# Attention products of a 3x3 convolution over 128 partitions, 5 for 6, with one read of x

## The reference

```python
x = x + L0(gn(x)); x = x + L1(gn(x)); x = x + L2(gn(x)); x = x + L3(gn(x))

def L0(x):                       # attention over channels, one head
    qkv = conv1x1(x, qkv_w)      # 48 -> 144 channels
    qkv = depthwise3x3(qkv, dw_w)
    q, k, v = split(qkv, 3)      # each (b, 48, h*w)
    q, k = l2_normalize(q), l2_normalize(k)
    attn = softmax(q @ k.T * temperature)      # 48 x 48
    return conv1x1(attn @ v, proj_w)
```

## Time and profile before

| | |
|---|---|
| median of 3 runs | 2777.19 us (2773.39 to 2782.19) |
| profiled execution | 2774.55 us |
| its span | 2772.4 us |
| TensorE busy | 2579.3 us (93%) |
| VectorE / ScalarE / GpSimd busy | 1492.3 / 1005.3 / 423.7 us |
| mean granted clock | 0.979 |

### The profile page before, as it was taken

How to read it: one execution, slowest core, us unless ns; L and a number is a source line. 1 busy time by engine, 2 the same in 40 slices (tenths; PEclk the granted TensorE clock), 3 DMA queues, 4 the chain that set the end, 5 groups by cost and what they waited for, 6 DMA issues and landing times.

```text
span 2772.4 us, 48058 instructions
## 1 busy us (share of the span) xinstructions
PE 2579.3 (93%) x18728; PEld 2244.8 (81%) x18728; DVE 1492.3 (54%) x3683; ACT 1005.3 (36%) x2608; POOL 423.7 (15%) x492
## 2 busy tenths in 40 slices
PE   1999999999999989999999998999999999877896
PEld 1999948954599559999999998999999999763443
DVE  3323323322333235677656787656776557876765
ACT  3524344354433334443344333344433443212221
POOL 1000000000300009400000235500000003563230
PEclk9999999999999999999999999999999999988998
DMA  8850000003000134000000436600000003657233
GB/s 150 146 87 4 1 0 1 1 1 87 4 1 1 23 68 48 2 2 1 2 1 2 92 64 121 92 1 1 2 2 1 2 2 70 169 136 219 79 103 91
DMA packets 245089, 130.32 MB, mean 47 GB/s; under 512 B 209152, under 2 KB 234080, under 8 KB 241856
## 3 DMA queue, kind: packets, MB, share of 16 engines
q1 hardware_dynamic: 243808, 126.52, 22.1%
q10 hardware_dynamic: 928, 0.76, 0.1%
q0 software_dynamic: 128, 0.01, 0.0%
HBM read 76.91 MB, written 50.33 MB: 46 GB/s over the span
## 4 chain that ended last, share of the span: by engine, by line
PE 84%; DVE 8%; SPq 2%; issue 2%; ACT 2%; DMA 1%; POOL 0%; ACTq 0%; DVEq 0%; POOLq 0%
PE bank L1057 16%; PE bank L1060 15%; PE bank L1058 15%; PE bank L950 14%; PE bank L1009 12%; PE bank L968 3%; PE bank L955 3%; PE bank L1199 2%; SPq L493 2%; PE bank L1141 1%; PE bank L1079 1%; DVE work L389 1%; DMA work<-in_x 1%; DVE stats L1222 1%; DVE bank L1416 1%
## 5 line engine op out<-in xcount | busy, mean ns | idle before, releaser
L1416 DVE TENSOR_SCALAR bank<-image,scan_bias 112x128 f32<-112x128 f32 x2032 | 706.9, 353 | 428.6 <-ACT image L809 400.6
L809 ACT COPY image<-bank 112x128 f32<-112x128 f32 x2032 | 546.1, 269 | 1031.8 <-PE bank L1060 920.2
L1057 PE MATMUL bank<-image,scan_wt 112*112 112x128 f32 x4064 | 810.5, 280 | 41.8 <-ACT image L809 39.6
L1058 PE MATMUL bank<-image,scan_wt 112*112 112x126 f32 x4064 | 770.7, 271 | 0.0
L1060 PE MATMUL bank<-image,scan_wt 112*112 112x126 f32 x4064 | 770.3, 270 | 0.0
L1057 PEld LDWEIGHTS bank<-image,scan_wt 112*112 112x112 f32 x4064 | 560.1, 175 | 98.9 <-ACT image L809 73.1
L1058 PEld LDWEIGHTS bank<-image,scan_wt 112*112 112x112 f32 x4064 | 581.2, 176 | 0.0
L1060 PEld LDWEIGHTS bank<-image,scan_wt 112*112 112x112 f32 x4064 | 578.6, 176 | 0.0
L755 ACT ACTIVATE work<-image,gn_shift,gn_scale 48x567 f32<-48x567 f32 (+3 forms) x384 | 335.1, 902 | 324.9 <-PE bank L955 202.2
L950 PE MATMUL bank<-work 112*128 112x192 f32 x2304 | 421.6, 331 | 10.1 <-issue 10.1
L950 PEld LDWEIGHTS bank<-work 112*128 112x128 f32 x2304 | 373.4, 192 | 11.6 <-issue 11.3
(11 more groups left out here) (140 smaller groups left out, 1516.9 us busy)
## 6 DMA issues: line engine op xcount, KB each, us to landing
work<-saved SPq DMA_DIRECT2D x64, 192.0 KB, 5.1
saved<-image SPq DMA_DIRECT2D x64, 192.0 KB, 4.0
work<-saved SPq DMA_DIRECT2D x128, 96.0 KB, 3.5
flat_rows<-work SPq DMA_DIRECT2D x64, 192.0 KB, 3.7
image<-flat_rows SPq DMA_DIRECT2D x4, 3072.0 KB, 14.5
out<-image SPq DMA_DIRECT2D x8, 1536.0 KB, 9.3
band<-in_x SPq DMA_DIRECT2D x16, 384.0 KB, 5.5
work<-in_x SPq DMA_DIRECT2D x16, 384.0 KB, 5.5
```

The source lines that it names most:

```text
L809: nc.scalar.copy(line(g, along_w, at), state_bank(g, done)).then_inc(s_state[g], 1)
L1057: mm(dst, wt[:, 1], src, start=False, stop=False, skip_group_check=True)
L1058: mm(dst[:, 1:J2, :], wt[:, 0], src[:, 0:J2 - 1, :], start=False, stop=False, skip_group_check=True)
L1416: v.tensor_scalar(state_bank(g, done), line(g, along_w, src), scan_bias[:, 3 * layer + kind:3 * layer + kind + 1], None, ALU.add).then_inc ...
```

## The change

- **128 partitions.** The spare partitions of `blk_z` get the n rows of channels 32 to 47, of both parities, by two DMAs a block on SP's queue (`tail`). They wait for `s_stage`, and their signal is `s_tail`.
- **Packed side columns.** `blk_2` holds the side columns of channels 0 to 31 for three rows on 96 partitions. For every block of every stage VectorE packs them in two turns (`pack(k, turn)`, five copies each), each after the near pieces of ScalarE (`s_near`) and with the signal `s_pack`.
- **Five products for six**: three over `blk_z` and two over `blk_2`. In QK0 that is 3 of 192 columns and 2 of 96 for 6 of 192; in QK1 to QK3 for 4 and 2; in CV 5 of 512 for 6.
- TensorE waits at a block's start for `s_stage`, `s_tail` and `s_pack` (`block_ready`). ScalarE writes the n pieces first, then the z pieces.
- **x is read once.** Six loads are started at once. For image 0 ScalarE copies the even and the odd part, for the others ScalarE the even and GpSimd the odd one. The norm of image 1 moves to the middle of QK0, that of images 2 and 3 into QK1. The small constants are spread behind the tails.

```diff
+        TAPS = [(LO, 0, 1), (slice(0, HALF), 1, 0), (slice(HALF, 128), 0, 2), (HI, 1, 1)]
...
+            def tail(k):
+
+                m = k % 2
+                sp.wait_ge(s_stage, k + 1)
+                sp.dma_start(blk_z[m][C:HALF, :], blk_n[m][SPARE, :]).then_inc(s_tail[m], 16)
+                sp.dma_start(blk_z[m][HALF + C:128, :], blk_n[m][HALF + 32:P, :]).then_inc(s_tail[m], 16)
...
+            for k in range(NBLK, 2 * NB * NBLK):
+                tail(k)
...
+                if k == CV_AT[1] + NBLK + 2:
+                    sp.wait_ge(s_x1, TWO + 2 * 2 * NBLK)
+                    for t in range(2):
+                        for half, rows in enumerate((LO, HI)):
+                            sp.dma_start(saved[0][half, :, t * IMG:(t + 1) * IMG],
+                                         image[rows, t * IMG:(t + 1) * IMG]).then_inc(s_save[t], 16)
...
             def split(c):
-                m, b, k0 = c % 2, c // LOADS, c % LOADS * BLK
-                act.wait_ge(s_load[m], 32 * (c // 2 + 1))
...
+                _, sem_at, n = rows_of(c)
+                act.wait_ge(s_load[sem_at], n)
+                last = nc.scalar.copy(*split_rows(c, False))
+                if c < LOADS:
+                    last = nc.scalar.copy(*split_rows(c, True))
+                last.then_inc(s_split, 1)
...
+                if i == 0 and k >= 2:
+                    act.wait_ge(s_pack, 2 * k - 2)
+                    act.wait_ge(s_tail[m], 32 * (k // 2))
+                elif i == 4:
+                    block_free(act, k)
+                sub, piece = i % 2, (1, 2, 0)[i // 2]
...
+            def block_ready(k):
+                pe.wait_ge(s_stage, k + 1)
+                pe.wait_ge(s_tail[k % 2], 32 * (k // 2 + 1))
+                pe.wait_ge(s_pack, 2 * k + 2)
...
+                    block_ready(first + n)
                     for sub in range(2):
 
                         pe.wait_ge(s_x1, b * 2 * NBLK + TWO + 2 * n + sub + 1 - len(banks))
-                        prods = [(buf, dy, s, dk) for buf in range(2) for dy, s, dk in conv_rows(sub)]
...
+                        for dy, s, dk in conv_rows(sub):
                             o = s * ZSUB + (1 + dk) * J2
...
+                            mm(dst, out_w[:, dy, :], blk_z[n % 2][:, o:o + BLK * J2], start=(dy == 0), stop=False)
+                            if beats is not None and dy != 1:
                                 beats()
+                        for side in range(2):
+                            last = mm(dst, out_w2[:, side, :], blk_2[n % 2][:, side, sub, :], start=False, stop=(side == 1))
+                        last.then_inc(s_conv, 1)
...
+            def pack(k, turn):
+
+                if k >= 2 * NB * NBLK:
+                    return
+                m, side = k % 2, 1 - turn
+                if turn == 0:
+                    block_free(dve, k)
+                dve.wait_ge(s_near, 2 * k + turn + 1)
...
+            def add_blocks(b, then):
                 for n in range(NBLK):
                     end = n == NBLK - 1
...
+                    for sub in range(2):
+                        last = add_part(b, n, sub, None if end else CV_AT[b] + n + 2, bank_out)
+                        if end and sub == 1:
+                            last.then_inc(s_stat, 1)
+                        pack(CV_AT[b] + n + 1, sub)
                     then(n)
```

More of the change, by code:

```diff
@@ L264, in build @@
         s_stage = sem("s_stage")
+        s_near = sem("s_near")
         s_pack = sem("s_pack")
+        s_tail = [sem(f"s_tail{m}") for m in range(2)]
         s_qk = sem("s_qk")
@@ L439, in _, with save_part @@
                         for m in shifts:
[L440 to L450, removed]
+                            small.append((scan_wt[rows, t, m + 1, cols], scan_w[t][:, 2 * m + qi - qo + 2, :], s_scan_c))
+            assert len(small) == N_GATE + N_SCAN_DMA
+            def save_part(i):
                 sp.wait_ge(s_x1, TWO + (NB - 1) * 2 * NBLK + (i + 1) * 2 * NBLK // PARTS)
@@ L729, in stage_piece @@
             def stage_piece(phase, n, i):
[L731 to L739, removed]
-                kk0, rows = 1 - sub, BLK + 1
[L741 to L748, removed]
+                b, m, k = ORDER[phase][1], n % 2, phase * NBLK + n
+                if i == 0 and k >= 2:
[4 more added lines that the diff above has]
+                sub, piece = i % 2, (1, 2, 0)[i // 2]
+                kk0, rows = 1 - sub, BLK + 1
+                outer = {0: 1, NBLK - 1: 0}.get(n)
+                if outer is not None:
+                    if i in (0, 4):
+                        o = outer * ZSUB + (0 if outer else BLK + 1) * J2
+                        nc.scalar.copy((blk_n, blk_z)[i // 4][m][0:P, o:o + J2], zero_row)
+                    if sub == outer:
+                        rows = BLK
+                        kk0 += n == 0
                 buf, part, d, e = ((blk_z, slice(0, P), (0, J2), (0, J2)), (blk_n, LO, (0, J2 - 1), (1, J2)),
@@ L938, in conv_pair @@
                     if i % 4 == 0:
-                        pe.wait_ge(s_stage, stages + (n + 1))
-                        if packed is not None:
-                            pe.wait_ge(s_pack, packed + (2 * n + 2))
+                        block_ready(first + n)
                     pe.wait_ge(s_qk_sb, pairs + (i + 1))
@@ L995, in tap_weights, with output_conv @@
                 for t in range(9):
-                    last = mm(bank_wt[0:P, t * C:(t + 1) * C], v_taps[:, t, :], mix_t, start=True, stop=True)
+                    last = mm(bank_wt[:, t * C:(t + 1) * C], v_taps[:, t, :], mix_t, start=True, stop=True)
                 last.then_inc(s_sm_t, 1)
-            def output_conv(b, stages, behind={}, banks=bank_out, beats=None):
+            def output_conv(b, first, behind={}, banks=bank_out, beats=None):
                 pe.wait_ge(s_outw, b + 1)
@@ L1001, in output_conv @@
                 for n in range(NBLK):
[L1002 removed]
+                    block_ready(first + n)
                     for sub in range(2):
                         pe.wait_ge(s_x1, b * 2 * NBLK + TWO + 2 * n + sub + 1 - len(banks))
[L1006 to L1007 removed]
+                        dst = banks[(2 * n + sub) % len(banks)][0:P, :]
+                        for dy, s, dk in conv_rows(sub):
```

336 lines of the change are left out of this document (203 added, 133 removed).

## The result

| | before | after |
|---|---|---|
| median | 2775.93 us (4 runs, 2773.39 to 2782.19) | 2809.11 us (4 runs, 2805.52 to 2817.29) |
| profiled execution, its span | 2774.55, 2772.4 | 2806.22, 2804.4 |
| TensorE busy | 2579.3 | 2495.5 |
| mean granted clock | 0.979 | 0.951 |

The ratio is 1.0119, 95% interval 1.0103 to 1.0134: the change made the kernel slower by 33 us. The prediction, 2770 with a range to 2806, had the sign wrong (about no change, leaning to faster) and missed the top of its range by 3 us. TensorE has 84 us less to do, and the kernel is longer all the same.

What follows compares the result with a forecast made beforehand. TensorE was taken to bound the kernel nearly everywhere. The terms -9.9 - 43.3 - 65.0 + 88.0 + 7 + 17.9 sum to -5.3 us on the profiled 2774.55, 2769.3; the forecast was 2770, range 2734 to 2806.

Steps and rivals of the forecast that it cites:

- A: Start, to TensorE's first product: x read once lets TensorE start at 47.2 us; -9.9 us (-5 to -14).
- B: QK0: cheaper products per pair, with a stall of 2 us at block 5; 117.0 against 160.3 us, -43.3.
- C: QK1, QK2, QK3: one product fewer per half pair, and QK1 loses its starting low clock; -65.0 us.
- D: CV0, CV1, CV2: TensorE idles 3.6 us a block for the pack and loses 1.9 to low clock; +88.0 us.
- E: Saving images 0 and 1: a tail that CV2's block 3 needs waits behind the save on SP's queue; +7 us.
- F: CV3: late beat 3 and idles of 4.0 us for the tail DMAs at six borders, then low clock; +17.9 us.
- Rival 4: CV stages: no stall, since VectorE gets the second pack done earlier; D would be -41, time 2641 us; 2%.
- rival 1: CV stages: the packs' wait costs only its length, the clock stays up; D +42, time 2714 us; 12%, parts included.
- rival 3: QK0: GpSimd's copies take VectorE's time, +14 us, with F +9 from DMAs of 4 us; time 2793; 13%.
- Rival 2: Low clock lasts twice as long behind each of the 30 stalls, +51 us, time 2821; 11%, parts included.

Runs made afterwards that it cites:

- The first experiment: The changed kernel with both turns of a block's pack moved ahead of the two adds in CV0 to CV2: 2683.64 us, ratio 0.9677.

## Why the prediction was wrong

The terms of the sum missed by 9.3 (A), 1.3 (B), 7.6 (C), 18.1 (D and E) and 1.1 (F), all in one direction; together 37.4, which is the whole way from -5.3 to +32.1.

**What held.** The mechanism of D was named as it is: the pack of the next block behind the add and the statistics of this block's second half, in each of 24 blocks, with a stall of the clock behind it. The first experiment shows it: with the order alone changed, the wait is gone and 125 us with it. B was off by 1.3 (the stall that I followed to block 5 is the 1.62 at 129.43), F by 1.1. Rival 4 is out, and so is rival 1: the clock was not free. That F came so near is partly luck. It had beat 3 of each block late by 0.9, and in the chain no beat of the block from 948.88 to 963.30 waits; against that the idle was 4.4 for 4.0, and the low clock cost more than 1.9 behind four of the six idles, where it lasted 6.8 us. A block takes 19.36 on the mean (948.88 to 1045.66, five of them) for the 19.3 forecast.

**The start, A (off by 9.3).** The step that failed is "With the same 4.8 us behind it, normalising starts at 35.9". It followed ScalarE's copies alone, which did end at 30.9; it did not ask what VectorE waits for ahead of its statistics. The constants on ScalarE's queue landed at 28.6, and the weights and all sixteen statistics came behind. The experiment on the order of the start gives the 9 back.

**D and E (113.1 for 95, off by 18.1).** These are four terms of one sign, and each is a size, not a mechanism. (1) The stall is 3.94 for 3.6: the copies take 2.20 for 2.14, and what lies between the five instructions and the two engines sums to 0.35, for which I had left 0.07. 24 x 0.34 = 8. (2) The low clock costs 2.0 a block in CV0 (116.05 less 8 x 8.59 and 8 x 3.94 leaves 15.8) and in CV1 and CV2 2.15 (252.7 less 16 x 8.59, 77.9 of idles and 3.0 of other small products leaves 34.4), for 1.9: 4.6 in sum. (3) The idle in front of block 3 is 13.34, so the save has 9.4 of it for 7: 2.4. (4) In CV2 GpSimd normalises an image while VectorE packs, and there the copies are slower. The timelines of VectorE and then of GpSimd there:

```profile
724.87 1.03 DVE L1417 COPY work<-work 32x1024 f32<-32x1024 f32 x1
725.91 2.41 DVE L1421 COPY work<-work 32x512 f32<-32x512 f32 x4
...
729.79 1.34 DVE L1417 COPY work<-work 32x1024 f32<-32x1024 f32 x1
```

```profile
724.56 11.20 POOL L650 TENSOR_SCALAR image<-image,gn_scale,gn_shift 112x512 f32<-112x512 f32 x11 [0.27 <-POOL image L650]
```

0.68 becomes 1.03 and 1.34, and four copies take 2.41 for 1.5. Two of the stalls were 6.25 and 5.04 for 3.94: 3.4. The four sum to 18.4, and small terms make up the difference to 18.1. The last would be rival 3's mechanism, in another stage than where I had put it. In QK0, where I had put it, GpSimd's copies took 1.14 at the median (I had 1.7), VectorE was busy for 90 of 118 us, and the stage kept its forecast. By the Trainium skill (SBUF — State Buffer, Who interferes with whom) of a copy that takes the shared ports and a GpSimd operation the one that comes first blocks the other; the longer copies of CV2 agree in kind. No run here takes GpSimd's work away, so the cause of these 3.4 us is not shown.

**C (-57.4 for -65.0, off by 7.6).** QK1 came out as worked, 116.5 for 115.7. The step that failed is that QK2 and QK3 lose nothing to what stands ahead of them. They begin with a low clock of 6.8 us, which is the second price of the last stall of CV0 and of CV2; it costs 3.3 in each, and with the packs first it is gone from QK2 (116.1 for 119.2). I had charged a stall's low clock to its own stage and had stopped at the stage's border.

**Rival 2, half true.** Twenty of the 24 stalls are idles of 3.83 to 3.97. At twelve of them the clock is low for some 3.4 us and at eight for some 6.8, though the idles are equal (303.84 and 318.29 above). The records show one thing that tells them apart. Of the following two stretches the first is the last piece of the idle ahead of 318.29, the second what comes behind it:

```profile
317.60:318.20 0.60, 0.00 (x0) 0.00 (x0) 0.44 (x2) 0.13 (x1) 0.00 (x0) 0.51 0.82 128
318.29:324.40 6.11, 6.11 (x8) 2.31 (x9) 0.00 (x0) 3.16 (x4) 0.00 (x0) 0.50 0.08 12
```

At the eight long ones the clock had fallen 0.7 to 2.2 us before TensorE started again, at the twelve short ones no more than 0.6 before, or up to 0.6 behind. Rival 2 had the 6.8 behind all of them and +51. Counted as above, what the longer ones add to my 1.9 is 4.6 in D and 6.6 in C, of 57 in all. The experiment with work in the stall bounds that price from below: 39.5 + 5. By the Trainium skill (TensorE: Matmul & The Clock Gate, HAM oscillation — how this bites in real kernels) a loop that waits long enough in each round is throttled in every round. The trace agrees: all 24 rounds of CV0 to CV2 had a low clock with a stall of 3.83 or more, and with 1.9 only some had.

**The errors had one sign.** I wrote that I had "rounded the stalls up throughout". In fact each was made of the durations of its instructions, with little for what lies between them, and for no stage did I ask for what the sum leaves out. A forecast between a gain of 118 and a loss of 113 has the errors of both, and five terms that each were a little short made -5 into +32. The range left the full form of rival 2 out, and of it about a fifth came, on top of sizes that were short.

**What stays open.** When within an idle the clock falls, and so why equal idles leave 3.4 or 6.8 us of low clock. Why the constants land so late: all that the trace shows is that they were issued from 4.96 to 7.8 us on while x came in on the other queue; no run moved them.

## What to carry to other kernels

A wait that a change adds is worth more than its length: read in the order of instructions what stands ahead of the signal on its engine, and put what the next block needs ahead of what the last block left; here that alone was 125 of 2809 us, with no work removed. When you take the last waiter away, write down who is late next and at what time, before you price the gain: in CV3 the DMA hid the pack, and half the gain went there. And when a forecast is a small difference of large terms, add up what each chain leaves between its instructions, since these errors don't cancel.

## What the runs showed of the hardware

- Equal idles of 3.94 us, repeated each 14.5 us on the mean, went with 3.4 us at a granted clock of 0.52 or with some 6.8 at 0.50; in the long ones the clock had fallen 0.7 us or more before TensorE started again. Repeated idles of 1.89 us went with a low clock in some rounds and with none in others (2.80 and 4.13 us for three products of 2.59). Idles of 0.88 us each 13.6 us left it at 1.00.
- The kernel with 16 more products a block was 39.5 us faster than without them; its granted clock was 1.00 through CV0 and CV1, where it was 0.86 in CV0 without them.
- A DMA of 0.2 KB issued at 7.4 landed after 21.2 us beside the loads of x, on another queue; one of 80 KB behind 6.3 MB on its own queue after 26.6, where the median of the 128 of its kind is 2.5.
